# Scores of an attention block: the second of two matmul passes on half of the partitions

## What is computed

```
q = (x @ Wq).reshape(B, N, HEADS, DIM_HEAD)
k = (context @ Wk).reshape(B, M, HEADS, DIM_HEAD)
v = (context @ Wv).reshape(B, M, HEADS, DIM_HEAD)
sim = einsum('bihd,bjhd->bhij', q, k) * SCALE
attn = softmax(sim, axis=-1)
out = einsum('bhij,bjhd->bihd', attn, v).reshape(B, N, INNER)
return out @ Wo + bo
...
x = x + tanh(g_xattn[0]) * xattn(layernorm(x), ctx, ...)
x = x + tanh(g_ffn[0]) * ffn(layernorm(x), ...)
```

## Time and profile before

| | |
|---|---|
| median of 3 runs | 1820.25 us (1819.62 to 1823.83) |
| span of the profiled execution | 1816.1 us |
| PE busy | 1794.9 us, 99% of the span |
| DVE / ACT / POOL busy | 1330.5 / 810.9 / 1184.1 us |
| chain that ended last, by engine | PE 96% |
| chain, share of the scores' matmuls (L696) | 5% |
| granted TensorE clock | 9 tenths or more in every slice |

### The profile page before, as it was taken

The page is one execution under the profiler, slowest core; times in us unless marked ns, Lnnn a source line. Parts: engine busy times, 40 slices in busy tenths (PEclk is TensorE's granted clock), DMA queues, the critical chain, the costliest instruction groups (busy, mean ns, idle before and its releaser), DMA issues.

```text
span 1816.1 us, 31801 instructions
## 1 busy us (share of the span) xinstructions
PE 1794.9 (99%) x9720; PEld 1615.8 (89%) x9720; DVE 1330.5 (73%) x2308; ACT 810.9 (45%) x1574; POOL 1184.1 (65%) x900
## 2 busy tenths in 40 slices
PE   7999999999999999999999999999999999999999
PEld 7999999999999878888888888888888888888887
DVE  7888878888888877666666766588766767676657
ACT  6767677677766832323232323243232323232322
POOL 5525445263544679777777777699877777777743
PEclk9999999999999999999999999999999999999999
DMA  5111202021120222111111111123412121212111
GB/s 176 39 41 36 57 22 61 21 62 40 34 69 16 92 97 74 66 54 62 58 58 58 58 58 58 47 66 106 127 57 63 52 69 47 69 46 69 46 47 53
DMA packets 52057, 110.35 MB, mean 61 GB/s; under 512 B 13208, under 2 KB 25496, under 8 KB 52000
## 3 DMA queue, kind: packets, MB, share of 16 engines
q1 hardware_dynamic: 52000, 109.64, 19.3%
HBM read 98.61 MB, written 11.01 MB: 60 GB/s over the span
## 4 chain that ended last, share of the span: by engine, by line
PE 96%; DVE 1%; issue 1%; ACT 1%; DMA 0%; SPq 0%; POOL 0%; ACTq 0%; DVEq 0%
PE bank L781 33%; PE scores L754 28%; PE bank L625 19%; PE scores L696 5%; PE bank L706 4%; PE bank L718 4%; PE bank L632 1%; PE scores L839 0%; DVE h_sum L1051 0%; DMA ctx_raw<-in_ctx 0%; ACT hs L1318 0%; PE bank L754 0%; ACT probs L1190 0%; DVE xs L900 0%; ACT h_full L1317 0%
## 5 line engine op out<-in xcount | busy, mean ns | idle before, releaser
L781 PE MATMUL bank<-w2s,hs 128*128 128x512 f32 x2688 | 620.9, 389 | 1.3 <-DVE xres L1018 1.0
L781 PEld LDWEIGHTS bank<-w2s,hs 128*128 128x128 f32 x2688 | 504.4, 188 | 105.1 <-issue 1.5
L754 PE MATMUL scores<-xs,w1s 128*128 128x448 f32 x2646 | 549.5, 366 | 3.6 <-DVE h_sum L1051 3.5
L754 PEld LDWEIGHTS scores<-xs,w1s 128*128 128x128 f32 x2646 | 495.8, 188 | 48.7 <-DVE h_sum L1051 3.8
L1051 DVE TENSOR_TENSOR h_sum<-scores,h_sum 128x448 f32<-128x448 f32 x441 | 262.7, 619 | 183.3 <-PE scores L754 182.8
L1317 ACT ACTIVATE h_full<-h_sum,b1T 128x448 f32<-128x448 f32 x256 | 170.9, 668 | 303.1 <-DVE h_sum L1051 292.4
L1066 DVE TENSOR_TENSOR acc<-bank,acc 128x512 f32<-128x512 f32 x337 | 229.1, 686 | 71.5 <-PE bank L781 62.9
L900 DVE TENSOR_TENSOR hs<-h_full,hs 128x448 fp32r<-128x448 f32 x256 | 237.9, 930 | 52.2 <-ACT hs L1318 52.1
L1190 ACT ACTIVATE h_sum<-scores 128x448 f32<-128x448 f32 x63 | 34.3, 545 | 475.4 <-PE scores L754 475.4
L1391 POOL TENSOR_SCALAR probs<-probs,row_inv 112x750 f32<-112x750 f32 x60 | 130.6, 2176 | 100.1 <-DVE row_inv L989 100.1
L1493 POOL CAST w1s<-w_stage 128x768 fp32r<-128x768 f32 x64 | 69.0, 1078 | 168.5 <-PE scores L754 168.5
(11 more groups left out here) (128 smaller groups left out, 2197.3 us busy)
## 6 DMA issues: line engine op xcount, KB each, us to landing
w_stage<-in_L_ffn_w SPq DMA_DIRECT2D x128, 512.0 KB, 3.5
ctx_raw<-in_ctx SPq DMA_DIRECT2D x16, 376.0 KB, 3.2
ctx_raw<-in_ctx SPq DMA_DIRECT2D x14, 374.0 KB, 3.2
xa<-in_x SPq DMA_DIRECT2D x16, 224.0 KB, 2.7
xres<-in_x SPq DMA_DIRECT2D x16, 224.0 KB, 2.7
x_scratch<-xres SPq DMA_DIRECT2D x16, 224.0 KB, 2.3
xt_scratch<-yT SPq DMA_DIRECT2D x16, 224.0 KB, 2.8
x_raw<-xt_scratch SPq DMA_DIRECT2D x4, 896.0 KB, 7.7
```

The source lines that it names most:

```text
L754: mm = pe.matmul(product_bank(g, name)[:, 0:TH], w1s[j % 2][:, s, W_OF[name], kc, :], xs[:, i, m, kc, :], start=n == 0, stop=n == 5)
L781: mm = pe.matmul(bank[:, :], hs[j % 2][:, s, ht, t * P:(t + 1) * P], w2s[j % 2][:, m, ht, :], start=n == 0, stop=n == 5)
```

## The change

It changes the layout of `keys` and the second pass of the scores. In the first run of keys nothing moves. In the second run (374 keys) the halves are swapped: the high parts lie in the 64 partitions that hold the low parts in the first run, and the other way round. The first pass (high queries, both parts of the keys) still goes over all 128 partitions, for both runs first. The second pass (low queries) now takes the high parts of the keys alone, so that it is a matmul over 64 partitions: the run of 376 uses one half of the partitions, the run of 374 the other half. The product of the low parts, low queries by low keys, is no longer part of the sum. The number of matmuls, their columns and the number of instructions on DVE and ACT stay what they were.

```diff
+def high_low(odd, half):
+    rows = [slice(0, 64), slice(64, 128)]
+    n = (odd + half) % 2
+    return rows[n], rows[1 - n]
...
                     for k0, k1 in HALVES:
-                        for s in range(2):
-                            last = pe.matmul(ps_scores[qt][0:QT, SCORES.start + k0:SCORES.start + k1],
-                                             qst[g][:, s, hh, rows], kst[g][:, hh, k0:k1], start=s == 0, stop=s == 1)
+                        pe.matmul(ps_scores[qt][0:QT, SCORES.start + k0:SCORES.start + k1],
+                                  qst[g][:, 0, hh, rows], kst[g][:, hh, k0:k1], start=True, stop=False)
+                    for half, (k0, k1) in enumerate(HALVES):
+                        high = high_low(hh % 2, half)[0]
+                        last = pe.matmul(ps_scores[qt][0:QT, SCORES.start + k0:SCORES.start + k1],
+                                         qst[g][high, 1, hh, rows], kst[g][high, hh, k0:k1], start=False, stop=True)
...
-                    sub(kst[g][64:128, 2 * p, keys], bank[0:64, 0:n], kst[g][0:64, 2 * p, keys])
-                    last = sub(kst[g][0:64, 2 * p + 1, keys], bank[64:128, 0:n], kst[g][64:128, 2 * p + 1, keys])
+                    for odd in range(2):
+                        src = slice(64 * odd, 64 * odd + 64)
+                        high, low = high_low(odd, half)
+                        last = sub(kst[g][low, 2 * p + odd, keys], bank[src, 0:n], kst[g][high, 2 * p + odd, keys])
...
-                    copy(kst[g][0:64, 2 * p, keys], bank[0:64, 0:n])
-                    last = copy(kst[g][64:128, 2 * p + 1, keys], bank[64:128, 0:n])
+                    for odd in range(2):
+                        src = slice(64 * odd, 64 * odd + 64)
+                        last = copy(kst[g][high_low(odd, half)[0], 2 * p + odd, keys], bank[src, 0:n])
```

## The result

The change is slower: 1844.59 us median (1843.34 to 1847.26) against 1820.16 us, a ratio of 1.0133 with a 95% interval of 1.0119 to 1.0147.

A forecast was written before the change was run, and what follows sets the result against it. PE was taken to bound the kernel; 0.37 us for two switches less 0.08 returned gave +0.29 us a step, x 128 = +37 us, so about 1857.4 us; forecast's own range 1844 to 1870, eight-in-ten range 1832 to 1872.

The forecast's parts named there:

- The two switches: PE, each score step: going from 128 to 64 partitions costs 0.18 us, coming back 0.19, together 0.37 us.
- What comes back: PE, each score step: second half-height matmul need not wait for the first; 0.08 us returned, leaving +0.29 us.
- the bounds: Three cases for PE per score step: nothing returns, +0.37 (+47 us); 0.08 returns, +0.29 (+37); 0.167 returns, +0.20 (+26).
- the row that I preferred: Profile row of step B, two loads 0.09 us apart; taken as the delay between the half-height matmuls' starts.
- The sum: Whole kernel: profiled span from 1816.1 to 1853.2 us, median from 1820.25 to about 1857.4 us.
- the bound of +26: PE, 128 score steps: second half-height matmul starts with the first, 0.167 us returns, +0.20 us a step.
- The idle end: Last batch: PE's idle time could swallow 3.6 us at most, left out; no wait behind score steps gets worse.
- Time around the span: Whole kernel: the median of the runs stands 4.15 us above the profiled span.
- The one without a drain: Rival, PE score steps: loads stay hidden, half-height matmuls run side by side, 19 us faster, 1801 us; chance 0.09.
- the one without any effect: Rival, PE score steps: no drain and no side by side, four matmuls of 0.171 us, 1820 us; chance 0.05.
- The smaller break: Rival, PE score steps: only one switch holds loads back or the drain is shorter, 1826 to 1843 us; chance 0.06.
- The layout: DVE's keys subtractions cross partitions in the second run: 0 to 4.4 us a batch on DVE, zero on the path.

The follow-up runs named there:

- the experiment: Changed kernel with the old layout of keys, so both half-height matmuls of a step use the same 64 partitions; 1873.13 us, ratio 1.0291.

## Why the prediction was right, and which term was off

**What bounds it.** PE was the bound in the loop, before and after: 80.44 of 80.44 us. Whatever a step lost was lost in full.

**The two switches.** Forecast 0.37 us a step from places where the tile goes to 16 and 8 partitions; the first load was to come 0.26 us after the second full matmul and came 0.26 us after it. The next load was to come some 0.25 us after the last half-height matmul started; the profile starts that matmul together with its load, so that the 0.35 us seen are 0.09 of open load and 0.26 from there. Four switches in a row cost 0.18 us each. The rows of narrower tiles priced a tile of 64 well, and the Trainium skill's rule that a change of tiling mode drains TensorE ("TensorEngine Tiling (Array Packing)", Key Properties) fits 64 rows too, with these 0.18 us; 80 partitions in a tile of 128 cost nothing.

**What comes back: this term was mis-sized.** For what returns when the second half-height matmul does not wait for the first, I took 0.08 us, because the two loads of step B follow each other by 0.09. But those are loads on the same partitions. On different ones they start within 0.01 us of each other, and so do the matmuls; on the same ones, in the experiment, they are 0.09 apart again. The whole matmul of 0.17 came back, which was the other end of the bounds, +0.20 a step. The Trainium skill's figure of 4 ns between such starts ("TensorE: Matmul & The Clock Gate", Part 3) fits these 0.01 us, and the row that I preferred was of another case.

**The sum.** With 0.17 back the sum would have been +26 us. Measured: 0.169 us a step in the loop, 21.6 us in all, and some 3 us more in the median (7.6 in the profiled execution, the slowest of the four). By single starts, a step with its open load behind takes 0.89 us, 0.20 more than before, so 0.03 us a step are saved elsewhere in the loop. The loads of the kernel before show where: over five batches, once a batch ahead of a transpose and once ahead of a step K, PEld stood idle.

```profile
PEld bank L706 <- issue: 2.1, 5, 0.4
PEld bank L625 <- issue: 1.4, 5, 0.3
```

With the change these two waits are gone, and the starts around them close up by about 0.5 us a batch, which is the 0.03 us a step. Of the 12.7 us between forecast and result, the mis-sized term is 11 (128 x 0.087). The result stands so near the bound of +26 by some luck, since these 0.03 us a step (4 us) and the 3 us that came on top nearly cancel.

**The idle end.** I had put the last batch aside with the remark that its idle time could only swallow something, and I had written that no wait behind S gets worse when PE is slower. In the loop that was so. In the last batch it went the other way: PE waited 2.29 us instead of 0.99 and then worked at half the granted clock. I had no term for DVE and POOL moving against each other.

**Time around the span.** I put 4.15 us around the span. All executions listed stand 2.0 us above their span; the other half was scatter, the profiled execution of before being one of the fastest. It does not touch the difference.

**Rivals.** The one without a drain is out in each step of the trace, and so is the one without any effect. The smaller break, whose range ends at 1843 us, close to the result, is out by its condition: both switches hold the load back, at 0.18 us each. The layout costs nothing, as said.

## What to carry to other kernels

Half-height matmuls do run side by side, and the second is free; but each change between tile heights on TensorE costs about one such matmul (0.18 us against 0.17), so two changes for one saved matmul lose and two for two break even. By these numbers only a longer run at one height could win, which no run here shows; two PSUM tiles of scores allow no more than two saved matmuls here. None of the variants beats the kernel before. To price an operation that the trace does not have, look for the nearest one that shares the resource in question: for a switch any narrow tile did, for two loads it had to be loads on different partitions.

## What had not been expected of the hardware

The load of a stationary operand can start with another one on other partitions: 256 loads, in pairs within 0.01 us. In the last batch the granted clock fell to 1.2 GHz around the end of a wait of 1.5 to 3.4 us on PE, or up to 2.4 us behind it, for 6.8 to 20.5 us, in all five kernels with half-height steps there, while the same place with a wait of about 1 us kept 2.4 GHz; yet a wait of 2.0 us near the end of the program was followed by a fall in one kernel and by none in another. And a DVE operation on 7 columns can take 2.27 us and end with the POOL operation beside it, as one on 896 columns can take 3.10 us instead of 1.08: work that is off the critical path came onto it because of when it ran.
